# The softmax maxima of the latent attention are turned and spread later, and the last batch's sums come ahead of them

## The reference

```python
x = layer_norm(x, ln_x_w, ln_x_b)                 # here x is the context
latents = layer_norm(latents, ln_l_w, ln_l_b)
q = latents @ Wq
kv_input = jnp.concatenate([x, latents], axis=1)  # 1556 rows
k, v = jnp.split(kv_input @ Wkv, 2, axis=-1)
...
q = l2norm(q) * q_scale
k = l2norm(k) * k_scale
sim = jnp.einsum('bhid,bhjd->bhij', q, k) * SCALE
sim = jnp.where(full_mask, sim, max_neg)
attn = jax.nn.softmax(sim.astype(jnp.float32), axis=-1).astype(sim.dtype)
out = jnp.einsum('bhij,bhjd->bhid', attn, v)
...
return layer_norm(out @ Wo, ln_o_w, ln_o_b)
```

## Time and profile before

| | us |
|---|---|
| median of 3 runs | 3767.55 (3767.08 to 3770.37) |
| the profiled execution | 3748.75, its span 3747.0 |
| TensorE busy | 3314.1 (88% of the span) |
| VectorE busy | 2529.9 (68%) |
| ScalarE busy | 2085.7 (56%) |
| GpSimd busy | 1150.4 (31%) |

### The profile page before, as it was taken

How to read it: one execution, slowest core, us unless ns; L and a number is a source line. 1 busy time by engine, 2 the same in 40 slices (tenths; PEclk the granted TensorE clock), 3 DMA queues, 4 the chain that set the end, 5 groups by cost and what they waited for, 6 DMA issues and landing times. The chain is left out here.

```text
span 3747.0 us, 96803 instructions
## 1 busy us (share of the span) xinstructions
PE 3314.1 (88%) x40678; PEld 2442.0 (65%) x40678; DVE 2529.9 (68%) x3627; ACT 2085.7 (56%) x3878; POOL 1150.4 (31%) x1140
## 2 busy tenths in 40 slices
PE   8786999999999678999999984689999999999989
PEld 5565677777777566777777762456666666666654
DVE  4653777777774346777777756578878787878751
ACT  3421566556664124656666654366777777676733
POOL 0024222222221352212222200145555545454530
PEclk8987999999999788999999997799999999999989
DMA  7934665565562336545455510100000000000000
GB/s 199 241 101 131 163 172 153 150 173 146 157 173 53 98 103 147 119 122 138 120 123 138 127 44 0 32 25 17 25 17 26 17 25 17 25 17 25 17 4 24
DMA packets 136408, 337.82 MB, mean 90 GB/s; under 512 B 56515, under 2 KB 78603, under 8 KB 135979
## 3 DMA queue, kind: packets, MB, share of 16 engines
q1 hardware_dynamic: 132843, 325.21, 33.6%
q0 software_dynamic: 3136, 6.46, 0.5%
HBM read 166.49 MB, written 17.17 MB: 49 GB/s over the span
## 5 line engine op out<-in xcount | busy, mean ns | idle before, releaser
L2148 POOL TENSOR_TENSOR l_S<-l_S,l_shift 125x448 f32<-125x448 f32 (+1 forms) x416 | 461.3, 1152 | 328.7 <-ACT l_shift L2380 326.2
L1464 ACT ACTIVATE L1a_probs<-ps 125x448 f32<-125x448 f32 x768 | 383.3, 544 | 204.1 <-PE ps L1364 190.6
L1464 ACT ACTIVATE L2a_probs<-ps 125x448 f32<-125x448 f32 x768 | 382.6, 544 | 203.2 <-PE ps L1364 189.6
L1497 DVE TENSOR_REDUCE L2a_chunk_max<-ps 112x1 f32<-112x1000 f32 x256 | 300.9, 1196 | 148.0 <-PE ps L1323 147.6
L1497 DVE TENSOR_REDUCE L1a_chunk_max<-ps 112x1 f32<-112x1000 f32 x256 | 300.9, 1196 | 137.3 <-PE ps L1323 136.8
L2361 ACT ACTIVATE ctx_stats<-ps 125x512 f32<-125x512 f32 (+1 forms) x416 | 247.9, 596 | 179.7 <-PE ps L2206 170.5
L2258 PE MATMUL ps<-l_S,l_z 125*128 125x448 f32 x768 | 344.2, 545 | 0.0
L2425 DVE TENSOR_REDUCE l_norms<-ctx_stats 125x8 f32<-125x512 f32 (+1 forms) x416 | 268.2, 676 | 77.1 <-ACT ctx_stats L2361 77.0
L2451 DVE SCALAR_TENSOR_TENSOR l_S<-ps,l_neg_cols,l_inv_norms 125x448 f32<-125x448 f32 x384 | 256.3, 680 | 81.4 <-PE ps L2227 76.5
L1323 PE MATMUL ps<-L1a_keys,L1a_queries 98*112 98x500 f32 x768 | 264.9, 428 | 47.5 <-DVE L1a_chunk_max L1497 20.8
L1323 PE MATMUL ps<-L2a_keys,L2a_queries 96*112 96x500 f32 x768 | 264.1, 426 | 46.3 <-DVE L2a_chunk_max L1497 20.7
(11 more groups left out here) (494 smaller groups left out, 7074.0 us busy)
## 6 DMA issues: line engine op xcount, KB each, us to landing
L1a_keys<-L1a_k_hi SPq DMA_DIRECT2D x256, 187.5 KB
L2a_keys<-L2a_k_hi SPq DMA_DIRECT2D x256, 187.5 KB, 3.7
L1a_ctx_T<-in_ctx_T SPq DMA_DIRECT2D x32, 750.0 KB, 6.3
xn<-L_valid SPq DMA_DIRECT2D x32, 750.0 KB, 7.8
L1a_keys<-L1a_k_lo SPq DMA_DIRECT2D x128, 187.5 KB
L2a_ctx_T<-in_ctx_T SPq DMA_DIRECT2D x32, 750.0 KB, 6.4
L2a_keys<-L2a_k_lo SPq DMA_DIRECT2D x128, 187.5 KB, 4.1
a_ctx_N<-in_ctx_N SPq DMA_DIRECT2D x32, 672.0 KB
```

Of the source, the lines that this page charges most:

```text
L1464: nc.scalar.activation(probs[t % NPR][:, h * HQ // 2:(h + 1) * HQ // 2], s.ps[0:KP, i % 3, 0:HQ // 2], ACT.Exp).then_inc(probs_made, 1)
L1497: ins = nc.vector.tensor_reduce(chunk_max[:, n, 0:1], product, AX.XY, ALU.max)
L2148: nc.gpsimd.tensor_tensor(S[b % 2][0:r, t, :], S[b % 2][0:r, t, :], shift[0:r, :], ALU.add)\
```

## The change

```diff
--- before.py
+++ after.py
@@ -2299,12 +2299,12 @@
                 for t in range(T):
                     if b + 1 < B:
                         key_product(b + 1, t)
-                    if t == 1 and b >= 0:
+                    if t == 3 and b >= 0:
                         turn_maxima(b)
-                    if t == 4 and b >= 0:
+                    if t == 2 and b >= 1:
+                        sums(b - 1)
+                    if t == 6 and b >= 0:
                         spread_maxima(b)
-                    if t == 5 and b >= 1:
-                        sums(b - 1)
                     if t == 7 and b + 1 < B:
                         queries_through_keys(b + 1)
                     if t == 9 and b >= 1:
@@ -2389,7 +2389,7 @@
                     act.wait_ge(heads_made, b)
                 nc.scalar.activation(mixed_lat[:, :], s.ps[:, 7, 0:HQ3], ACT.Copy).then_inc(lat_mixed, 1)
 
-            EARLY = 6
+            EARLY = 5
             normalize(0)
             take_context(0)
             for b in range(-1, B):
@@ -2398,7 +2398,7 @@
                 for t in range(T):
                     if b + 1 < B:
                         square(b + 1, t)
-                    if t == 5 and b >= 0:
+                    if t == 7 and b >= 0:
                         take_shift(b)
                     if t == 8 and b + 1 < B:
                         take_queries(b + 1)
@@ -2522,11 +2522,11 @@
             for b in range(-1, B):
                 if b >= 1:
                     mix(b - 1)
-                if b >= 0:
-                    maxima(b)
                 for t in range(T):
                     if b + 1 < B:
                         reduce_squares(b + 1, t)
+                    if t == 2 and b >= 0:
+                        maxima(b)
                     if t == 6 and b >= 1:
                         invert_sums(b - 1)
                     if t == 8 and b + 1 < B:
```

## The result

The changed kernel takes 3882.45 us (median of 4 runs, 3877.15 to 3886.16) against 3767.32 us before: a ratio of 1.0319, 95% interval 1.0300 to 1.0339, slower. The profiled execution took 3881.54 us, its span 3879.8. The busy times on the page of the profile have hardly moved.

A forecast was written before the change was run, and what follows sets the result against it. A ring through TensorE, ScalarE and GpSimd, closing every 36.97 us, was taken as the bound. Ring 67, last iteration 1.5 and clock 36 gave +104 us, 3872 us; range 3830 to 3890.

The forecast's parts named there:

- The ring: Loop chain of shift copy, subtractions, last exponential, normalizing, transposes, next start: 36.97 us, to grow 2.3 us, 67 us in all.
- The stall: TensorE's wait for `z` ahead of the next context's transposes: to grow from 0.64 to about 3.1 us.
- The new wait of the sums: On TensorE behind key product 2, the sums wait for VectorE's copy `l_mixed`: about 1.0 us.
- EARLY = 5: One exponential moved behind ScalarE's square root: counted at nothing under its wait for GpSimd, up to 0.5 us without.
- The clock: TensorE's clock halves behind the longer wait for `z`: 1.58 us a fall, in 7/9 of 29 iterations, 36 us.
- The likeliest case: Loop's chain longer and TensorE's clock falling in most iterations: +104 us, 3872 us, chance 0.50.
- the rival with a fall in nearly every iteration: TensorE's clock falls in nearly all loop iterations: +117 us, 3885 us, chance 0.17.
- The ends: Iteration 0 counted at nothing, as `z` has room; last iteration 1.5 us longer, with copy and sums on the path.
- The rival on the other side: Not slower: GpSimd's idle time ahead of the subtractions takes up the later shift; 3763 us, chance 0.06.
- the slack of `z`: At TensorE's wait for `z`: 2.3 us of slack needed for no slowdown; rows show a 0.64 us stall instead.

The follow-up runs named there:

- stall filled: Changed kernel with eleven unused products on TensorE ahead of its wait for z: period 39.33 us, ratio 1.0215.
- the spread sooner: Changed kernel with the spread behind key product 5 instead of 6 and the shift copy behind square 6 instead of 7: period 38.67 or 40.4 us, ratio 1.0209.
- changed kernel with z early: Changed kernel with ScalarE's normalizing ahead of the last five exponentials instead of behind them: period 37.01 us, ratio 1.0011.
- z early in the kernel before: Kernel before with ScalarE's normalizing ahead of the last four exponentials: period 36.33 us, ratio 0.9965.

## Why the prediction was right

3882.45 us is 10 us above the forecast of 3872 and within the range of 3830 to 3890. The mechanism, a longer ring and a clock that falls behind the longer stall, is what the runs showed; the rate of the falls was too low, and small errors at the two ends of the loop of −2.7 and +0.9 us cancel in part.

- **The ring.** I had the shift copy at 10.31 us of the iteration; it starts at 10.32. I took 2.3 us for the growth; it is 2.37 (stall filled). The stall, foretold as about 3.1 us, is 3.11. That GpSimd and ScalarE's order are links of it is shown by cutting the subtractions (−1.90 us) and by taking `z` out from behind the exponentials (−3.95 us with the clock).
- **The new wait of the sums**: 0.90 us where I had 1.0.
- **EARLY = 5**, which I counted at nothing under GpSimd's cover and at up to 0.5 us without: 0.36 us without it, by itself. That it is nothing under the cover follows from the last exponential's start, 0.04 us behind GpSimd's end; it was not run with EARLY = 6.
- **The clock.** The size, 1.58 us a fall, was right: 1.63. The rate was not: 29 of 29, where I took 7 of 9 from the trace. What was off is the step from scattered stalls, most of them in other stages, to a rate in a loop that repeats itself. That term is 47 us instead of 36. The likeliest case in name was the wrong one of two neighbours; the rival with a fall in nearly every iteration, 3885 us, is what happened, at 3882.
- **The ends.** Iteration 0 went from 2455.00 → 2495.41 to 2465.03 → 2502.72 us, 2.7 us shorter, where I had nothing: I wrote that `z` had room there, but TensorE's waits of 3.16 us for the scores and 1.41 us for the tops are gone, and a wait of 1.40 us for `z` and one of 1.85 us for the squares stand instead. The last shift copy is 2.4 us later against the start of iteration 30, where I had 1.5; which part of it is longer was not taken apart.

The sum by the two traces: −2.7 + 29 × 4.0 + 2.4 = 116 us in the loop, 69 of it the ring and 47 the clock. I had 104, of 67, 36 and 1.5. The medians differ by 115. The spans differ by 133: 10 us lie ahead of iteration 0 and 7 behind the last shift copy, in stages that the change does not touch and that differ as much between other kernels' traces.

The rival on the other side, that GpSimd's idle time takes up the later shift, fell where I said it would be decided, at the slack of `z`. It becomes true once `z` stands ahead of the exponentials.

## What to carry to other kernels

An engine with two thirds idle time can be a link in the ring that sets a loop's period; find the ring by matching ends and starts over all engines (here two gaps of 0.05 us), and ask of each moved instruction whether it lies in it. When a wait is moved out of the way, look at what stands in order behind the last link: here moving the twelve normalizing instructions ahead of a few exponentials made both the old stall and the new delay free. A stall of TensorE can cost a second time, by the clock: here 1.63 us or 2.85 us on top of a stall of 3.1 us. In iterations 1 to 29 of this loop stalls of 2.6 us and more did it, those up to 1.65 us did not. That is no safe limit: of ten kernels with a stall of 1.85 us in iteration 0, nine showed a fall 0.9 to 1.6 us behind it, and in an earlier stage of the kernel before the clock fell behind a stall of 1.66 us.

## What the runs showed of the hardware that I had not expected

- In a steady loop the falls of the clock come in a pattern and not like draws at a rate. With a stall of 3.1 us they came in 29 of 29 iterations of one kernel and 24 of 29 of another, there without a break from b = 12 on; with 2.6 us in 19 of 29, nearly always in a rhythm of two falls and one without. Two kernels with rings of 39.33 and 38.1 us locked to the same period of 40.96 us, one with 3.4 us at half clock per iteration, the other with 6.8 (0.8 of it in the stall). Wherever two iterations in a row had a fall, in all three kernels, the two falls lay 40.96 us apart, but for one pair of 37.55; with the spread sooner too, where the two stalls ended only 40.3 us apart. So the fall is not set off at a fixed time behind the stall, and the loop keeps step with the falls. What sets the distance was not settled.
- TensorE's idle stretch could be filled with useless products at no cost that the period shows: eleven of them took 47 us out of the loop.
- VectorE's raise with both operands in SBUF and GpSimd's split stand for each other completely: 1.65 us instead of 0.61 when GpSimd began 0.09 us sooner, 0.62 when it began 0.40 us later. In the kernel before and in the changed one VectorE began first by 0.1 to 0.4 us in nearly every iteration. That order, which no line of the code asks for, was worth 0.8 us an iteration in the changed kernel with z early. The longer raise does not always cost: at 1.38 us, with z early in the kernel before, TensorE did not wait for it.
